# Product-key experts: the expert weighting moves from VectorE to GpSimd, and the next input's scaling and half of its similarities move ahead of the last two one-hot chunks

## The reference, cut to what matters

```python
# h: [32, 113, 256]; layer norm, then inside _L3_ffn_ref:
xn = _rmsnorm(x, norm_w)
q = (xn @ w_q.T).reshape(b, t, 8, 2, 128)
sim1 = einsum('bthd,hkd->bthk', q[..., 0, :], keys[:, :, 0, :])   # 8 heads x 64 keys
sim2 = einsum('bthd,hkd->bthk', q[..., 1, :], keys[:, :, 1, :])
s1, i1 = top_k(sim1, 8); s2, i2 = top_k(sim2, 8)
# best 8 of the 64 sums per head -> 64 chosen experts of 4096 per token
fs, pk = top_k(all_sc, 8); fi = take_along_axis(all_idx, pk)
hidden = gelu(einsum('btd,bthkd->bthk', xn, expert_down[fi]))
hidden = hidden * relu(fs)
return einsum('bthk,bthkd->btd', hidden, expert_up[fi])           # added to h
```

## Time and profile before

| what | value |
|---|---|
| median of 3 runs | 5304.43 us (5295.95 to 5305.81) |
| the profiled execution, its own time | 5299.59 us |
| its span, first to last instruction | 5297.9 us |
| PE busy | 4556.0 us, 86% |
| DVE busy | 3690.1 us, 70% |
| ACT busy | 2142.8 us, 40% |
| POOL busy | 2509.7 us, 47% |
| granted TensorE clock, mean | 0.929 of full |

### The profile page before, as it was taken

The page is one execution under the profiler, slowest core; times in us unless marked ns, Lnnn a source line. Parts: engine busy times, 40 slices in busy tenths (PEclk is TensorE's granted clock), DMA queues, the critical chain, the costliest instruction groups (busy, mean ns, idle before and its releaser), DMA issues. The chain is left out here.

```text
span 5297.9 us, 65263 instructions
## 1 busy us (share of the span) xinstructions
PE 4556.0 (86%) x22344; PEld 2899.1 (55%) x22344; DVE 3690.1 (70%) x7355; ACT 2142.8 (40%) x4025; POOL 2509.7 (47%) x1494
## 2 busy tenths in 40 slices
PE   7888599768888888888885999896998899999999
PEld 4555267533333333333332546793445788888888
DVE  4764222268889888988987323214885999999997
ACT  3654011135555555555553223233663232233322
POOL 3441400279999999999995000000221443334333
PEclk8998799879899999999987999897998899999999
DMA  2003123322222222222221000571002000000000
GB/s 71 1 1 110 59 69 121 114 68 71 70 68 71 67 71 67 71 67 71 68 70 52 0 6 1 222 275 37 1 1 84 3 5 5 5 3 5 5 5 5
DMA packets 153112, 287.22 MB, mean 54 GB/s; under 512 B 24441, under 2 KB 135024, under 8 KB 144206
## 3 DMA queue, kind: packets, MB, share of 16 engines
q1 hardware_dynamic: 144926, 263.59, 15.2%
q0 software_dynamic: 6656, 14.04, 0.8%
q10 hardware_dynamic: 1200, 5.42, 0.3%
HBM read 252.33 MB, written 33.42 MB: 54 GB/s over the span
## 5 line engine op out<-in xcount | busy, mean ns | idle before, releaser
L1509 PE MATMUL ssm_ps<-ssm_hc,net_ident 128*128 128x452 f32 x2048 | 961.8, 596 | 190.9 <-DVE ssm_hc L1765 105.9
L1691 POOL TENSOR_TENSOR ssm_dBu<-ssm_du,ssm_bc 128x904 f32<-128x904 f32 x512 | 1064.6, 2100 | 3.2 <-POOL ssm_du L1709 1.7
L1610 ACT ACTIVATE ssm_ps<-ssm_step,ssm_decay 128x448 f32<-128x448 f32 x1024 | 647.6, 636 | 645.9 <-DVE ssm_ps L1755 435.9
L1509 PEld LDWEIGHTS ssm_ps<-ssm_hc,net_ident 128*128 128x128 f32 x2048 | 392.5, 204 | 726.2 <-issue 347.3
L1755 DVE TENSOR_TENSOR_SCAN ssm_ps<-ssm_ps,ssm_dBu 128x452 f32<-128x452 f32 x512 | 565.1, 1104 | 131.6 <-POOL ssm_dBu L1691 45.2
L1755 DVE TENSOR_TENSOR_SCAN ssm_hs<-ssm_ps,ssm_dBu 128x452 f32<-128x452 f32 x512 | 551.4, 1077 | 41.4 <-ACT ssm_ps L1610 37.0
L1702 POOL TENSOR_TENSOR ssm_hc<-ssm_hs,ssm_bc 128x904 f32<-128x904 f32 x256 | 537.8, 2101 | 74.4 <-DVE ssm_hs L1755 74.4
L3139 POOL TENSOR_TENSOR peer_hot_parts<-peer_hot_cols,peer_parts 128x1024 bf16<-128x1024 bf16 (+1 forms) x240 | 433.8, 1810 | 127.1 <-DVE peer_hot_cols L3157 114.2
L2995 PE MATMUL peer_ps<-peer_xn,peer_down 128*128 128x226 f32 x2048 | 447.4, 365 | 0.0
L3064 PE MATMUL peer_ps<-peer_hid,peer_up 128*128 128x226 f32 x2048 | 398.2, 354 | 1.6 <-DVE peer_hid L3191 1.6
L3064 PEld LDWEIGHTS peer_ps<-peer_hid,peer_up 128*128 128x128 f32 x2048 | 388.9, 190 | 6.5 <-issue 2.2
(11 more groups left out here) (425 smaller groups left out, 8059.5 us busy)
## 6 DMA issues: line engine op xcount, KB each, us to landing
ssm_bc<-ssm_rows SPq DMA_DIRECT2D x256, 452.0 KB, 3.6
ex_w<-in_l_ffn_w SPq DMA_DIRECT2D x64, 1024.0 KB, 6.6
moe_w_gu<-in_moe_gate_up SPq DMA_DIRECT2D x16, 704.0 KB
slots_in<-rt_zeros SPq DMA_DIRECT2D x17, 640.0 KB, 8.6
moe_rows_in<-slots_in SPq DMA_DIRECT2D x16, 512.0 KB
slots_out<-xp_rows_out SPq DMA_DIRECT2D x16, 512.0 KB
moe_w_dn<-in_moe_down SPq DMA_DIRECT2D x16, 384.0 KB
peer_down<-in_peer_down_t SPq DMA_DIRECT2D x1, 4096.0 KB, 17.9
```

Source lines behind the costliest of these rows:

```text
L1509: nc.tensor.matmul(Y_BANK[j][:, 0:GT], c["ident"][:, :], hc[:, q % 2, j, :], start=False, stop=(n == S - 1))\
L1610: nc.scalar.activation(rows(dA(i % 2))[:, :, lo:lo + N - 1], rows(step[hf.d][:, j, :])[:, :, lo:lo + N - 1], ACT.Exp, scale=decay[hf.d][:, ...
L1691: nc.gpsimd.tensor_tensor(dBu[:, q % 2, j:j + 2, :], du[hf.d][:, j:j + 2, :], bc[:, q % RING, 0:1, :].to_broadcast([P, 2, GT]), ALU.mult). ...
```

## The change: what it does

Three edits inside `peer`, all in the hand-written order:

1. The 16 weighting instructions leave VectorE's stream and stand in GpSimd's, behind the step's last `hot_parts`, with the same waits (`gelu_done`, `evac_done`).
2. `scaled_input(k + 2)` on VectorE, with its wait on `hid_mm`, moves from behind chunk 14 to ahead of chunk 13.
3. `similarities` takes a batch `b`. The four products of batch 0 are issued between `weights(k, 12)` and `weights(k, 13)`, those of batch 1 where all eight stood.

```diff
-        def similarities(pe, k):
+        def similarities(pe, k, b):
...
-            for b in range(PB):
-                for half in range(2):
-                    for m in range(DK):
...
+            for half in range(2):
+                for m in range(DK):
...
                         for ch in range(HU - LAG if k else 0, NC):
+                            if ch == NC - 2 and fronts[k] is not None:
+                                pe.wait_ge(s["gelu_done"], (k + 1) * HU)
+                                similarities(pe, k + 1, 0)
                             weights(k, ch)
...
                         if fronts[k] is not None:
-                            similarities(pe, k + 1)
+                            similarities(pe, k + 1, 1)
...
+                        pool.wait_ge(s["gelu_done"], (k + 1) * HU)
+                        pool.wait_ge(s["evac_done"], (k + 1) * NC)
+                        for i in range(HU):
+                            block_ = hid[:, i * J:(i + 1) * J, :]
+                            nc.gpsimd.tensor_tensor(block_, block_, weight[:, i * J:(i + 1) * J, :, :].rearrange("p j b n -> p j (b n)"),
+                                                    ALU.mult).then_inc(s["wgt_done"], 1)
...
                         for ch in range(NC):
+                            if ch == NC - 2 and fronts[k] is not None:
+                                dve.wait_ge(s["hid_mm"], (k + 1) * HU)
+                                scaled_input(dve, k + 2)
                             one_hot(k, ch)
-                        if fronts[k] is not None:
-                            dve.wait_ge(s["hid_mm"], (k + 1) * HU)
-                            scaled_input(dve, k + 2)
                         if afters[k] is not None:
                             norm.vector_centre(nc, dve, h[:, :, afters[k]], k + 3)
-                        dve.wait_ge(s["gelu_done"], (k + 1) * HU)
-                        dve.wait_ge(s["evac_done"], (k + 1) * NC)
-                        for i in range(HU):
-                            block_ = hid[:, i * J:(i + 1) * J, :]
-                            nc.vector.tensor_tensor(block_, block_, weight[:, i * J:(i + 1) * J, :, :].rearrange("p j b n -> p j (b n)"),
-                                                    ALU.mult).then_inc(s["wgt_done"], 1)
```

More of the change, by code:

```diff
@@ L2958, in similarities @@
                 pe.wait_ge(kq_done, 4)
-            for b in range(PB):
-                for half in range(2):
-                    for m in range(DK):
-                        mm = nc.tensor.matmul(ps[first + 2 * b + half][0:N, :], xn[:, m, b * N:(b + 1) * N],
-                                              kq[:, m, half * 512:(half + 1) * 512], start=(m == 0), stop=(m == DK - 1))
-                    mm.then_inc(s["sim_mm"], 1)
+            for half in range(2):
+                for m in range(DK):
+                    mm = nc.tensor.matmul(ps[first + 2 * b + half][0:N, :], xn[:, m, b * N:(b + 1) * N],
+                                          kq[:, m, half * 512:(half + 1) * 512], start=(m == 0), stop=(m == DK - 1))
+                mm.then_inc(s["sim_mm"], 1)
         def codes_turned(pe, k):
@@ L3034, in _ @@
                     second_moment(pe, 1)
-                    similarities(pe, 0)
+                    for b in range(PB):
+                        similarities(pe, 0, b)
                     pe.wait_ge(big_in, 32)
```

## The result

The changed kernel took 5344.10 us, the median of 4 runs (5334.92 to 5345.83), against 5304.97 for the kernel before: a ratio of 1.0072, 95% interval 1.0060 to 1.0085. It is slower by 39 us. Predicted were 5334 and a range of 5306 to 5360.

What follows compares the result with a forecast made beforehand. TensorE's chain was taken to bound the kernel, with VectorE's weighting hidden. Steps 1 to 13 lose 1.85 us each (24.1); with the other three, 32.5 on 5299.59; forecast 5334 us, allowing for the median, range 5306 to 5360.

Steps and rivals of the forecast that it cites:

- VectorE is near the path but not on it: End of a step: VectorE's codes are ready 0.18 us before TensorE turns them, so relieving VectorE alone shortens nothing.
- Scaled input ahead of chunk 13: VectorE waits for the last hidden group, then scales in 0.82 us; chunk 13 and all behind it come 2.48 us late.
- Batch 0's similarities in the hole: Half the similarities, 3.5 us, fit ahead of `weights` 13; worth 1.0 us a step if the blocks are ready.
- A block on GpSimd costs 1.140, a block per 1.095: GpSimd's weighting product: 1.140 us each, 1.095 back to back, slower than the 0.77 in which TensorE eats a block.
- the two families of rows: GpSimd's profile rows at 452 columns: 1.140 us with two distinct full operands, 0.939 with a repeated one; the first was taken.
- The hindrance: VectorE's norm scaling and first pair sums slow GpSimd's weighting: 0.6 us a step, bounds 0 and 1.3.
- The first half ends 19.2 behind the last evacuation: Expert-up's first half, paced by GpSimd: ends 18.62 us plus 0.6 hindrance behind the last evacuation, where it was 19.85.
- The other steps: Steps outside 1 to 13: the first +2 us (bounds 0 and 4), the one before last +2.4, the last +4.0.
- Cheap blocks: Rival: GpSimd's product takes 0.895 us a block, steps 1 to 13 gain 1.0 each, 5286 us; 10 in 100.
- Dearer blocks: Rival: VectorE hinders GpSimd in every block, 1.19 us each, 1.6 more in each of 16 steps, 5357 us; 10 in 100.
- The clock: Rival: TensorE, pausing 0.3 us in each of the first half's last blocks, could be granted a lower clock; 4 in 100.

Runs made afterwards that it cites:

- Order alone: Changed kernel with the weighting back on VectorE, early scaled input and split similarities kept; ratio 1.0061 to the kernel before, 77.02 us a step.
- Half the blocks' columns: Changed kernel with each GpSimd block product over one of its two tiles, half the weighting left out; ratio 0.9975 to the kernel before, 73.97 us a step.
- Scaled input alone: Kernel before with only the scaled input moved ahead of chunk 13; ratio 1.0101 to the kernel before, 78.59 us a step.
- One operand: Changed kernel with each GpSimd block multiplied by itself in place, expert weight left out; 73.97 us a step, single execution of 5223.02 us (kernel before: 5230.56).
- GpSimd alone: Kernel before with only the weighting moved to GpSimd, scaled input and similarities where they were; ratio 1.0008 to the kernel before, 75.20 us a step.
- Split at the same time: Changed kernel with blocks 12 to 15 on VectorE behind its centring, last step all on VectorE; ratio 1.0059 to the kernel before, 77.08 us a step.
- Split in turn: Split at the same time, but GpSimd weights blocks 0 to 3 during VectorE's batch-0 searches, then VectorE the rest; ratio 0.9976 to the kernel before.

## Why the prediction was right, point by point

- **VectorE is near the path but not on it.** Right. The 8.72 us taken from it became 3.4 us of lying codes and 4.7 us of waiting for the root. Order alone shows how near: VectorE came 2.4 us later, TensorE without the wait would have come some 1.0 earlier, and TensorE waited 2.95 us.
- **Scaled input ahead of chunk 13: 2.48 us.** 2.40: the wait was as said, and the two instructions freed the engine after 0.73, not 0.82. The last evacuation came 6.47 us behind the last hidden group's semaphore, against 4.07.
- **Batch 0's similarities in the hole.** Right: they end before `weights` 13 can start, and Half the blocks' columns gives the worth of edits 2 and 3, 1.0 to 1.1 us a step. What I had not seen is that without them the hole costs clock as well (Scaled input alone).
- **A block on GpSimd costs 1.140, a block per 1.095.** Measured 1.141; in the last step, with VectorE idle, 16 took 17.59 us, which is one per 1.097. The choice between the two families of rows was the weightiest of the working, and One operand shows it to be right: the second full operand, not writing in place, makes it slow (1.141 us, and 0.937 with one address, both in place). One reading was wrong: L2610, the source of the upper bound of 1.19, squares a tile in place, so both operands are one address, and its quickest took 0.930 us. It belongs to the cheap family, and its mean of 1.239 was no bound for this product.
- **The hindrance: 0.6, bounds 0 and 1.3.** 0.88 (18.47 against 17.59), inside. It sits in two blocks of each of steps 1 to 13, the sixth and the eleventh, beside the norm's scaling and the pair sums as the prediction said; they took 1.53 and 1.59 us, the others 1.14.
- **The first half ends 19.2 behind the last evacuation.** 19.35. Step: 2.40 + 19.35 - 19.85 = +1.90, predicted +1.85. (The working writes 0.1 + 16 x 1.095 as 17.52, which is the 16 blocks alone; its next sum, 18.62, has the 0.1 in it.) That the two agree to 0.05 is in part luck: the hindrance was put 0.28 too low, but the late chunk 0.08 too high, and TensorE moved on 0.05 us behind the last block where 0.23 was reckoned.
- **The other steps.** The first +2.6 (said 2), the one before last +2.95 (2.4), the last +3.95 (4.0). The rows for it are the last step's, before and after:

```profile
5279.95 0.39 DVE L3199 TENSOR_TENSOR net_h<-net_h,peer_ps 128x226 f32<-128x226 f32 x1 [6.08 <-PE peer_ps L3064]
```
```profile
5306.40 0.79 ACT L3088 ACTIVATE peer_weight<-peer_ps 128x512 f32<-128x512 f32 x2 [1.82 <-PE peer_ps L3011]
5307.33 17.59 POOL L3150 TENSOR_TENSOR peer_hid<-peer_hid,peer_weight 128x452 f32<-128x452 f32 x16 [1.72 <-ACT peer_weight L3088]
5326.05 0.39 DVE L3202 TENSOR_TENSOR net_h<-net_h,peer_ps 128x226 f32<-128x226 f32 x1 [21.48 <-PE peer_ps L3067]
```

  The first half's result is added 14.91 us behind the last evacuation before, 18.86 after. All 16 together are +34.4 where 32.5 were predicted. The medians moved by 39.1, which leaves 4.7 us beyond the 16 steps of the two profiled executions; their cause stays open.
- **The rivals.** Cheap blocks: One operand and Half the blocks' columns give just its 74.0 us a step, but not at this price of a block. Dearer blocks: a single block took 1.193 us in the mean, but they overlap, and 18.47 us for 16 is one per 1.15; the surplus comes from two stretched blocks a step, not from all, and those were in the sum as the hindrance. The clock: TensorE's granted clock was 1.00 from step 1 to step 13, so the eight waits of 0.2 to 0.9 us in each first half did not lower it.

## What to carry to other kernels

Moving work off an engine pays only where that engine is waited for; find the next waiter first, and ask what rate the consumer eats at, since a slower producer that starts early enough is all but free (GpSimd alone: 0.25 us a step) and the same producer with its cover taken away is not (the changed kernel: 1.9). Price an elementwise product on GpSimd from a row with as many distinct full operands as the new one has, not from one of the same columns: 452 columns took 1.141 us with two operands and 0.937 with one address for both. And give GpSimd its two-operand work where VectorE reads PSUM: with 4 blocks on GpSimd beside VectorE's searches the whole was 0.24% faster than before; with 12 on GpSimd and VectorE's 4 in the middle of them it was 0.59% slower, and GpSimd's blocks alone took 2.5 us longer a step.

## What the runs showed of the hardware that I had not expected

- On GpSimd the same product of 128x452 f32 took 1.141 us with two tiles and 0.937 with one address for both operands. With two tiles, 226 columns took 0.663.
- VectorE's product of two SBUF tiles took 1.56 us instead of 0.62 beside GpSimd's train of such products, and the six of VectorE's two-tile instructions in that train (four blocks, the scaling, the pair sums) cost GpSimd 15.61 - 13.1 = 2.5 us, 0.4 each; in the changed kernel two of them cost 0.88. In Split at the same time VectorE's median block took 0.94 us more, somewhat less than a GpSimd block's 1.14, and GpSimd's blocks beside them 1.52 us instead of 1.14. And the one that was slowed was not always VectorE: in the changed kernel its scaling took 0.70 us, little more than 0.62, while GpSimd's block beside it took 1.53. By what rule the two give way to each other is not shown.
- A pause of TensorE of 3.98 us was followed by a stretch at a granted clock of 0.50 in each of the 13 steps of Scaled input alone, at an estimated 1.2 us a step; in Order alone one began within 1.2 us of the end of the pause of 2.95 us ahead of the turned codes, in 8 of 13. Such stretches also stand behind a shorter pause. In the kernel before, TensorE pauses 1.83 us near the start of the chunks, and in 4 of the 13 steps a stretch at 0.50 begins 1.0 to 1.4 us behind that; in Half the blocks' columns and Split in turn it is every third step. One of them, in the kernel before:

```profile
4784.30:4787.70 3.40, 3.40 (x22) 2.92 (x21) 3.37 (x4) 1.06 (x2) 2.85 (x2) 0.50 0.01 2
```

  There it costs little: such a step of Half the blocks' columns took 74.10 us, the others 73.92. The eight waits of 0.2 to 0.9 us in the changed kernel's first half, and the pause of 1.59 us ahead of `weights` 13 in the kernel before, had no low stretch behind them in any of the 13 steps. What decides in which steps the clock falls is not shown.
